# Layer 1's mixed steps on one Trainium2 core: work moved from VectorE to GpSimd and ScalarE, and the causal corner zeroed instead of masked by products

## The reference

```python
h = _layernorm(x) * (1 + ca) + sa                      # first pass
x = x + ga * _L1_attn_ref(h, ...)                      # bias attention with a gate
h = _layernorm(x) * (1 + cb) + sb                      # second pass
x = x + gb * _L1_ffn_ref(h, ...)
# _L1_attn_ref
scores = jnp.einsum('bqhd,bkhd->bhqk', q, k) * scale + _tisa_bias(...)
weights = jax.nn.softmax(scores, axis=-1)
attn = jnp.einsum('bhqk,bkhd->bqhd', weights, v)
a, g = jnp.split(out @ w_gate + b_gate, 2, axis=-1);   return a * jax.nn.sigmoid(g)
# _L1_ffn_ref
x = x + _mla(_rmsnorm(x, g1), ...)                     # causal attention:
scores = jnp.where(causal, scores, -1000000000.0);     a = jax.nn.softmax(scores, axis=-1)
x = x + _moe(_rmsnorm(x, g2), ...)                     # 8 experts, the top 2 of each token
```

## Time and profile before

| | us |
|---|---|
| median of 3 runs | 1864.76 |
| lowest, highest | 1862.15, 1874.69 |
| the profiled execution | 1861.73 |
| its span | 1860.0 |

### The profile page before, as it was taken

The page is one execution under the profiler, slowest core; times in us unless marked ns, Lnnn a source line. Parts: engine busy times, 40 slices in busy tenths (PEclk is TensorE's granted clock), DMA queues, the critical chain, the costliest instruction groups (busy, mean ns, idle before and its releaser), DMA issues.

```text
span 1860.0 us, 50554 instructions
## 1 busy us (share of the span) xinstructions
PE 1617.7 (87%) x19264; PEld 1179.7 (63%) x19264; DVE 1326.5 (71%) x4176; ACT 1007.1 (54%) x2196; POOL 779.3 (42%) x1021
## 2 busy tenths in 40 slices
PE   3899898899883939989999999989999988888887
PEld 2677676777772727766666666656767766544545
DVE  6678777876761127788778798897886786685646
ACT  1545454455451316665666667666666656564532
POOL 3111311220115237786656566565464574243210
PEclk7899999999995969999999999999999999988999
DMA  3631122122004424344423325143452333535321
GB/s 111 190 94 46 40 84 65 36 69 82 5 7 122 157 81 155 131 151 151 160 64 128 125 84 164 56 147 98 131 161 88 114 127 111 161 98 162 109 62 53
DMA packets 143839, 194.53 MB, mean 105 GB/s; under 512 B 21920, under 2 KB 110176, under 8 KB 142320
## 3 DMA queue, kind: packets, MB, share of 16 engines
q1 hardware_dynamic: 129312, 171.75, 29.6%
q0 software_dynamic: 5760, 14.03, 2.4%
q10 hardware_dynamic: 8528, 5.51, 1.0%
HBM read 142.39 MB, written 50.69 MB: 104 GB/s over the span
## 4 chain that ended last, share of the span: by engine, by line
PE 44%; DVE 9%; issue 7%; ACT 5%; DMA 1%; POOL 1%; SPq 0%; another core or an unknown queue 0%; ACTq 0%; POOLq 0%; DVEq 0%
PE ps L2350 9%; PE ps L2333 7%; PE ps L2384 6%; PE ps L2394 3%; DVE l_XY L2601 3%; PE ps L2361 3%; ACT PT L2162 2%; PE ps L1229 2%; PE ps L2484 2%; PE ps L1238 2%; PE ps L2459 2%; PE ps L2410 2%; DVE ps L2601 1%; PE ps L2431 1%; PE ps L2522 1%
## 5 line engine op out<-in xcount | busy, mean ns | idle before, releaser
L2053 POOL TENSOR_SCALAR l_XY<-l_XY,l_nmax 128x512 f32<-128x512 f32 x512 | 374.9, 737 | 295.9 <-DVE l_nmax L2601 287.6
L2601 DVE CUSTOM_DVE_ANT_0 l_XY<-ps,strips 128x512 f32<-128x512 f32 x512 | 347.7, 687 | 170.4 <-PE ps L2333 115.2
L2162 ACT ACTIVATE PT<-ps 128x512 f32<-128x512 f32 x512 | 307.3, 601 | 248.0 <-PE ps L2350 236.3
L2333 PE MATMUL ps<-l_stack 72*128 72x512 bf16 (+3 forms) x1024 | 350.9, 348 | 50.1 <-DVE l_nmax L2601 35.5
L2350 PE MATMUL ps<-ident,l_XY 128*128 128x128 f32 x2048 | 320.6, 279 | 1.7 <-ACT PT L2162 1.4
L2350 PEld LDWEIGHTS ps<-ident,l_XY 128*128 128x128 f32 x2048 | 236.9, 142 | 91.0 <-issue 56.8
L2601 DVE CUSTOM_DVE_ANT_0 ps<-ps,mask 128x384 f32<-128x384 f32 (+3 forms) x512 | 250.2, 496 | 24.3 <-PE ps L2333 20.2
L2361 PE MATMUL ps<-l_stack 75*128 75x256 bf16 (+3 forms) x512 | 157.2, 308 | 22.0 <-ACT PT_odd L2165 7.5
L2333 PEld LDWEIGHTS ps<-l_stack 72*128 72x128 bf16 x1024 | 101.1, 99 | 100.5 <-DVE l_nmax L2601 55.7
L2384 PE MATMUL ps<-PT,v_aug 128*10 128x128 f32 x4096 | 137.6, 275 | 6.8 <-ACT l_O_sb L2171 6.4
L2165 ACT ACTIVATE PT_even<-ps 128x512 f32<-128x512 f32 (+1 forms) x256 | 125.1, 494 | 22.8 <-PE ps L2363 17.3
(11 more groups left out here) (372 smaller groups left out, 3215.9 us busy)
## 6 DMA issues: line engine op xcount, KB each, us to landing
l_stack<-parts_dram SPq DMA_DIRECT2D x384, 96.0 KB
strips<-bias_dram SPq DMA_DIRECT2D x16, 1792.0 KB
stack<-parts_dram SPq DMA_DIRECT2D x48, 384.0 KB
w_own<-table_dram SPq DMA_DIRECT2D x60, 256.0 KB
parts_dram<-l_parts SPq DMA_DIRECT2D x32, 384.0 KB
rows_dram<-mask SPq DMA_DIRECT2D x6, 2048.0 KB, 8.9
parts_dram<-parts SPq DMA_DIRECT2D x16, 384.0 KB, 6.5
x_b<-rows_dram SPq DMA_DIRECT2D x72, 64.0 KB
```

What stands on the lines that cost most here:

```text
L2053: nc.gpsimd.tensor_scalar(XY[:, c % XY_BUFS], XY[:, c % XY_BUFS], -1.0, nmax[:, c % 8:c % 8 + 1], ALU.mult, ALU.add).then_inc(y_pool, 1)
L2162: nc.scalar.activation(PT[:, u % QUADS, j], src.rearrange("p (k q) -> p k q", q=P), ACT.Exp).then_inc(moved, 1)
L2333: nc.tensor.matmul(ps[:, n % 3, 0:w], stack[0:STACK, 0, h, q * P:(q + 1) * P], stack[0:STACK, 1, h, 0:w], start=True, stop=True).then_inc( ...
L2601: nc.vector.tensor_tensor_reduce(out=dst, in0=src, in1=add, scale=-1.0, scalar=3.0e38, op0=ALU.add, op1=ALU.min, accum_out=low).then_inc(s ...
```

## The change

**Mask products.** `scores_turned` makes one product instead of two. A new GpSimd function `causal(u)` zeroes the corner of four exponentiated tiles at once, two steps after the last of them was turned, and `values_turned` waits for it (`masked`).

**Off VectorE.** The adds into x of both passes go to GpSimd (`x_added`, `x_gated`). A split's subtract and cast become one subtract that writes bfloat16, and GpSimd takes the subtract that is left, ahead of its last part (not for batch 0). The scalings of xn in the second pass and of xf in the routers of batches 0 to 5 go to ScalarE, as four 128x128 activations each. Normalising and the two row operations of the second pass become two sets of four 128x128 products with a row as third operand.

**Moved.** The y0 products of batch b go from step 3 to the last steps of the pass before (57 and 61), the add to step 0, normalising to 13, its turn from 14 to 15; the splits to 24 and 27. The row for them is loaded at step 20 instead of 60. Router stages and the plan of the blocks move by one or two steps, mostly to remainder 1 (mod 4).

```diff
-MIXED_STAGES = dict(wo=1, add=3, square=5, var=8, power=9, scale=15, turn=17, logits=19, top0=21, top1=25, both=25, gap=27, count=28,
-                    place=37, gates=37, scatter=38, plan=(50, 52, 54, 56, 58), fold=41)
+MIXED_STAGES = dict(wo=1, add=4, square=6, var=9, power=10, scale=13, turn=17, logits=19, top0=21, top1=25, both=25, gap=27, count=28,
+                    place=37, gates=37, scatter=38, plan=(45, 49, 53, 55, 57), fold=41)
...
+def pre_step(b, stage):
+
+    if b == 1:
+        return {"y0": 3, "y1": 5, "x": 7, "statistics": 9, "var": 11, "power": 12, "xn": 13, "split": 24}[stage]
+    return TILES * (b - 1) + {"y0": -7, "y1": -3, "x": 0, "statistics": 5, "var": 9, "power": 10, "xn": 13, "split": 24}[stage]
...
+def causal_at(m):
+
+    return [u for u in range(BIAS // 4) if turned_step(1, 4 * u + 3) + 2 == m]
...
+                def causal(u):
+
+                    wait_moved(pool, ("T", (1, 4 * u + 3)))
+                    late = turned_keys(u % 4)[:, :, 0:P]
+                    nc.gpsimd.affine_select(out=late, in_=late, compare_op=ALU.is_ge, fill=0.0, base=0,
+                                            pattern=[[0, 4], [1, P]], channel_multiplier=-1).then_inc(masked, 1)
...
+                def x_added(b):
+                    pool.wait_ge(y_scaled, E + b)
+                    nc.gpsimd.tensor_tensor(x_rows(b), x_rows(b), y0[:], ALU.add).then_inc(x_in, 1)
+
+                def x_gated(b):
+                    pool.wait_ge(mid_sum, E + b + 1)
+                    nc.gpsimd.tensor_tensor(x_rows(b), x_rows(b), h_of(b), ALU.add).then_inc(x_mid, 1)
...
                 def last_part(k, a, b):
                     pool.wait_ge(second_part, 2 * PART_NO[a, b] + k + 1)
+                    if PART_NO[a, b]:
+                        order.link(nc.gpsimd.tensor_tensor(qk[:, k, :], qk[:, k, :], parts[:, k, 0, :], ALU.subtract))
                     nc.gpsimd.tensor_tensor(parts[:, k, 2, :], qk[:, k, :], parts[:, k, 1, :], ALU.subtract).then_inc(parts_ready, 1)
...
+                    if s in MID_OF and i == 43:
+                        b = MID_OF[s]
+                        act.wait_ge(rstd_ready, VARIANCES[2, b] + 1)
+                        for t in range(TT):
+                            last = nc.scalar.activation(xn[:, t, :], h_of(b)[:, t, :], ACT.Copy, scale=rstd[2][:, t:t + 1])
+                        last.then_inc(tok_scaled, 1)
...
+                        if k == routing(b)["scale"]:
+                            act.wait_ge(rstd_ready, VARIANCES[3, b] + 1)
+                            for t in range(TT):
+                                last = nc.scalar.activation(xf[:, t, :], h_of(b)[:, t, :], ACT.Copy, scale=rstd[3][:, t:t + 1])
+                            last.then_inc(tok_scaled, 1)
...
                         pe.wait_ge(max_stacked[buffer], 16 * MAXIMA[g])
                     nc.tensor.matmul(ps[:, to, 0:T - k * P], stack[:, 1, h, k * P:(k + 1) * P], stack[:, 0, h, k * P:T],
-                                     start=True, stop=False)
-                    nc.tensor.matmul(ps[:, to, 0:P], ident_b[:], mask_turned[:], start=False, stop=True).then_inc(turned, 1)
+                                     start=True, stop=True).then_inc(turned, 1)
...
-                    wait_moved(pe, ("T", (1, 4 * u + 3)))
+                    pe.wait_ge(masked, u + 1)
...
                     if part == 0:
-                        s = PART_NO[a, b]
                         wait_moved(dve, (("pq", "pk", "mq", "mk")[2 * a + k], b))
-                        link(nc.vector.tensor_tensor(qk[:, k, :], qk[:, k, :], parts[:, k, 0, :], ALU.subtract))
+                        if PART_NO[a, b]:
+                            nc.vector.tensor_tensor(parts[:, k, 1, :], qk[:, k, :], parts[:, k, 0, :], ALU.subtract).then_inc(second_part, 1)
+                        else:
+                            link(nc.vector.tensor_tensor(qk[:, k, :], qk[:, k, :], parts[:, k, 0, :], ALU.subtract))
...
+                        dve.wait_ge(var_ready, VARIANCES[1, b] + 1)
+                        for t in range(TT):
+                            last = nc.vector.scalar_tensor_tensor(out=h[:, t, :], in0=x_tile(b, t), scalar=mean_var[1][:, t, 0:1],
+                                                                  in1=mid_rows[:, 2], op0=ALU.subtract, op1=ALU.mult)
...
+                        dve.wait_ge(rstd_ready, VARIANCES[1, b] + 1)
+                        for t in range(TT):
+                            last = nc.vector.scalar_tensor_tensor(out=h[:, t, :], in0=h[:, t, :], scalar=rstd[1][:, t:t + 1],
+                                                                  in1=mid_rows[:, 1], op0=ALU.mult, op1=ALU.add)
```

131 lines of the change are left out of this document (72 added, 59 removed).

## The result

| | before | after |
|---|---|---|
| median us (lowest to highest, 15 runs each, same chip) | 1869.49 (1860.52 to 1874.69) | 1878.14 (1869.73 to 1890.70) |
| ratio of the runs | | 1.0053 (95%: 1.0036 to 1.0070) |
| mean granted clock of TensorE | 0.95 (profiled execution) | 0.938 (median of the runs) |
| profiled execution, span | 1860.0 | 1888.9 (the slowest of the 15) |

The change made the kernel 9 us slower, where 40 us less were forecast and the range ended at 1854.

The account below looks back on a forecast made before the run. It took the mixed stretch as bound by TensorE's streaming plus about 42 us in which VectorE is late. Terms: -13.5 - 4.5 - 30 - 1 + 3 + 6 = -40 us, from 1861.7 to 1821.7 profiled, median 1824; range 1797 to 1854.

Parts of the forecast that it names:

- (b): VectorE in the mixed stretch: 35 us less work and 17 us moved end 30 us of TensorE's 42.4 us of waits.
- (a): TensorE's 512 mask products, 57 ns each: removal gains 13.5 us in the mixed stretch and 4.5 us later.
- I take two thirds: Mixed stretch: of 20 us of mask products, two thirds, 13.5 us, counts as time, where TensorE is waited for.
- 70% of the waits are time: Mixed stretch: of 42.4 us that score products' weight loads wait for VectorE, 70% is taken as gained, 30 us.
- The loss of 1 to 5 us: VectorE's remaining operations, mixed stretch: more GpSimd work on the shared port pair slows them by 1 to 5 us.
- (c): ScalarE, mixed stretch: 11 blocks of four scalings at 306 ns each, 13.4 us of work, cost 3 us.
- (d): GpSimd's new zeroings, adds and subtracts cost 6 us: 4 in crowded steps, 1 each in bias-only and late stretches.
- has some 1.92 us of its own: GpSimd's zeroing of a unit's last tile: 0.6 us of work has a 1.92 us step before value products need it.
- The second one: Relief spent elsewhere, on waits for ScalarE and late negated tiles: gain of only 15 us, 1849 us; chance 0.18.
- The first: Rival that nearly all waits vanish, at little cost: -69 us, so 1795 us; chance 0.14.
- The third: GpSimd becomes the bound in the mixed stretch once a zeroing takes 2.5 us; 1888 us at 3.2 us; chance 0.07.
- the first one read: Sign in the changed profile's mixed stretch: score products' weight loads wait about 13 us for VectorE instead of 42.

Follow-up runs that it names:

- c1: Changed kernel with splits and scalings back on VectorE, expert rows loaded earlier and the router's old steps; ratio to the kernel before 0.9917.
- e6: Changed kernel with the rows of the expert blocks loaded 5 steps (first group) and 1 step (second group) earlier; ratio to the kernel before 1.0072.
- e9: Changed kernel with only the table of the router's steps as before; ratio to the kernel before 1.0036.
- c5: c1 with the 11 additions to x back on VectorE too; ratio to the kernel before 0.9913.
- b2: Kernel before without its 512 mask products and nothing in their place (causal scores not masked); ratio to the kernel before 0.9962.
- e2: Changed kernel with the mask products back on TensorE and no zeroing on GpSimd; ratio to the kernel before 1.0079.
- c2: c1 with the mask products back on TensorE and no zeroing; ratio to the kernel before 0.9921.
- e7: Changed kernel with the 11 blocks of scalings back on VectorE, in the same steps; ratio to the kernel before 1.0083.
- e1: Changed kernel with GpSimd's zeroing right behind the negation of the same step instead of ahead of it; ratio to the kernel before 1.0085.
- e4: Changed kernel without any causal mask, neither products nor zeroing (causal scores not masked); ratio to the kernel before 1.0039.
- c4: c1 without any causal mask, neither zeroing nor products (causal scores not masked); ratio to the kernel before 0.9891.
- e5: Changed kernel with the split of the q and k parts as before, subtract and rounding on VectorE; ratio to the kernel before 1.0032.
- a_again: The changed kernel once more, unaltered, against the kernel before; ratio 1.0061, span of its profiled execution 1876.2 us.
- e8: Changed kernel with the 11 additions to x back on VectorE, in the same steps; ratio to the kernel before 1.0081.

## Why the prediction was wrong, point by point

The step that failed most is (b): that 35 us of work taken off VectorE, and 17 moved, end 30 us of waits. The sum was -40 us, the kernel lost 9. Of the 35 us, the splits, the additions and the scalings are 32. With splits and scalings put back on VectorE (c1, together with the edits of e6 and e9) the kernel was 25 us faster than the changed one; with the additions put back too (c5) nothing changed that can be measured. What these moves brought instead of time were waits for GpSimd, ScalarE and SyncE's queue.

**(a) Mask products, -13.5 and -4.5.** The 57 ns a product is right (the median by which a step of b2 is shorter where TensorE nowhere stands), the share of it that is time was mis-sized. b2 measured 7 us (4 to 10) in place of 18. The step that failed is "I take two thirds": where 20 us of products had been, the two rows of waits for VectorE (which partly cover the same time) grew by 32 us, and steps 136 to 508 became 8.6 us shorter; over the whole kernel 7 of 29 us of products were time, a quarter. The text had named the cause (a faster TensorE "runs into VectorE sooner") and priced it only under (b).

**(b) VectorE's relief, -30.** The work left as costed, to within 1 us. With the products in place, the score products' waits did fall by 32 us (e2), but the mixed steps took 8 us longer than before, as waits for others came in. Two things were wrong. The sum of waits was read from the weight loads alone (42.4 us) and left 28.2 us of the products' own row out. And "70% of the waits are time" had no support: c2, which keeps relief and gives back the rest, has 26 us less of these waits and gained 12 us in the stretch. With the products out too, the waits came back to 50.0 + 16.9 us, so (a) and (b) were counted as a sum where they share one slack. The loss of 1 to 5 us left inside this term did not show: a split's subtract on VectorE, which now writes bfloat16, took 833 ns, before 848, with GpSimd busy 0.69 of the stretch.

**(c) ScalarE, +3.** Each scaling took 393 ns, not 306, and in step 43 of five passes TensorE stood about 1.0 us for it (7.7 to 8.7 us at step 232, gone in e7): 5 us. The same kind of burst, the router's four squares, was moved one step out from behind the value products, by a table that the prediction passed over as "moved". It cost 0.8 us in each of four passes (gone in e9): another 3 us. The term should have been about 8.

**(d) GpSimd, +6.** The durations were right. The claim that a zeroing "has some 1.92 us of its own" held for the value products, but GpSimd's slack behind VectorE went with it, where 0 was priced: 9 us against no mask at all (e1 and e4; behind the negation), 0.26%, 5 us, between c1 and c4, whose intervals overlap; in their traces steps 136 to 508 differ by 8.6 us. The subtracts were priced at their crowding on GpSimd; their real path was not followed. In bias-only steps they cost 1.4 and 1.7 us at two places, with a lower clock behind the second in some kernels (1 us forecast, gone in e5). In steps 412 to 424 they delay the second half of the parts, its store, and in the same queue of SyncE 12 loads and the expert rows: 5.4 us (gone in e5 and e6). The prediction follows no store or load of SyncE's queue.

**The clock.** No term of the sum had it. Over the runs the granted clock went from 0.95 to 0.938, and in the mixed stretch of the profiled execution that is 22 us of TensorE's speed, as much as the products gave (0.98 in a_again, about 15 us). At two places the loss can be read as time, against kernels that wait alike at the full clock: 1.6 us in steps 96 to 100 and 4 us in 368 to 376. The rest can't be split from the waits around it.

**The rivals.** The second one, the relief spent elsewhere on ScalarE and late negated tiles, had the mechanism, at 1849 us and 0.18; it still came to a gain of 15 us, where 9 were lost, since it lacked the queue of SyncE and the clock. (The first, at 1795, lies just outside the stated range of 1797 to 1854, which was said to take it in; nothing here hangs on it.) The third, GpSimd the bound from 2.5 us a zeroing, was rightly unlikely: a zeroing took 0.65. The tests named at the end did their work: the first one read, 42 us to 13, stood at 50.

## What to carry to other kernels

When an engine that is waited for and the one that waits are both relieved, count the slack between them once, and don't take a removed instruction for its duration: here 512 products were worth a quarter of theirs. Follow every moved operation to the last thing behind it: what is queued after it on its engine, and after its store or load on the DMA queue; a small subtract can be late by 3 us and cost 5 elsewhere. Move bursts on ScalarE or GpSimd only into steps where the engine they feed has a long piece of work, and judge a repair by its steps in the trace as well as by the ratio of whole runs: single ones did not show in the ratio, and all four together gave 1.3%.

## What was not expected of the hardware

- In the 6 us around a wait of 5.38 us for a DMA the granted clock was 0.78, in the next 6 us 0.65. But it fell as well after waits of 0.58 and 0.86 us (before, step 424), and of two kernels with the same waits of 0.66 and 0.47 us in steps 368 to 376 one (after) ran these steps at 0.79 and one (e6) at 1.00. Three per cent of clock over the mixed stretch (22 us) equal the 20 us that the removal of 353 products took off TensorE.
- At the same place the DMA engines were busy for 6 us at 352 GB/s, and a load of two rows issued in front of that took 9.1 us, where TensorE in the kernel before went on 7.6 us after the issue, and that for another engine's sake. In e6 such loads landed 1.7 to 3.6 us after their issue.
- The same instructions ahead of layer 1 took from 686.6 to 692.1 us in the profiled executions of e5 to e8, on one chip. That is as much as e6 and e7 mended in their places (7 and 5 us), which showed no gain in the ratio; the four repairs together showed 25 us.
